# Sums of local attention weights: overlapping columns added on GpSimd before TensorE sums them, with a new time table

## The reference

```python
# local: a query at j looks at keys j-32 .. j+31
logits = jnp.where(win & valid, q . k * scale, NEG)
out_local  = softmax(logits) @ v
# global: each query looks at every 64th key (128 of them)
out_global = softmax(q . k[:, ::64] * scale) @ v[:, ::64]
out = (out_local + out_global) @ w_out + b_out
```

## Time and profile before

| | |
|---|---|
| median of 3 runs | 3730.59 us (3727.56 to 3732.28) |
| the profiled execution | 3731.16 us, span 3728.6 us |
| mean granted clock of PE over the span | 0.991 of full speed |
| PE / DVE / ACT / POOL busy in the span | 98% / 62% / 43% / 52% |
| PE matmul pieces | 28480 |
| attention phase | begins at about 1220 us |

### The profile page before, as it was taken

How to read it: one execution, slowest core, us unless ns; L and a number is a source line. 1 busy time by engine, 2 the same in 40 slices (tenths; PEclk the granted TensorE clock), 3 DMA queues, 4 the chain that set the end, 5 groups by cost and what they waited for, 6 DMA issues and landing times.

```text
span 3728.6 us, 77177 instructions
## 1 busy us (share of the span) xinstructions
PE 3652.7 (98%) x28480; PEld 2682.6 (72%) x28480; DVE 2318.0 (62%) x5354; ACT 1596.2 (43%) x3110; POOL 1938.8 (52%) x3091
## 2 busy tenths in 40 slices
PE   8999999999998899999999999999999999999997
PEld 6888888888886567766667666666766666666665
DVE  4333333333334577777777777777777777777774
ACT  3222222222222355555555555555555555555553
POOL 0000000000000477777777777777777777777776
PEclk9999999999998999999999999999999999999999
DMA  4554554554457666666666666666666666666641
GB/s 146 203 189 160 191 198 163 179 202 171 167 211 185 131 141 144 139 145 152 151 141 141 141 150 150 144 140 143 150 146 145 141 149 147 141 145 143 150 111 40
DMA packets 420883, 571.20 MB, mean 153 GB/s; under 512 B 41656, under 2 KB 187208, under 8 KB 420568
## 3 DMA queue, kind: packets, MB, share of 16 engines
q1 hardware_dynamic: 412024, 564.79, 58.0%
q10 hardware_dynamic: 8256, 2.16, 0.3%
q0 software_dynamic: 288, 0.08, 0.0%
HBM read 361.59 MB, written 203.23 MB: 151 GB/s over the span
## 4 chain that ended last, share of the span: by engine, by line
PE 63%; POOL 1%; ACTq 1%; ACT 0%; DVE 0%; issue 0%; POOLq 0%
PE ps_misc L1056 19%; PE ps_max L974 10%; PE ps_sc L996 6%; PE ps_o L1028 6%; PE ps_max L977 5%; PE ps_s L1028 4%; PE ps_sc L1010 4%; PE ps_o L1040 3%; PE ps_s L1034 3%; PE ps_sc L1065 1%; ACTq L842 1%; PE ps_sc L983 1%; PE ps_sc L1004 1%; ACT qk L819 0%; POOL rsb L752 0%
## 5 line engine op out<-in xcount | busy, mean ns | idle before, releaser
L885 DVE TENSOR_REDUCE mx<-ps_max 128x2 f32<-128x256 f32 (+1 forms) x1365 | 485.5, 356 | 494.2 <-PE ps_max L977 471.0
L819 ACT ACTIVATE qk<-ps_sc 128x384 f32<-128x384 f32 (+1 forms) x1024 | 419.3, 461 | 669.1 <-PE ps_sc L996 662.3
L451 PE MATMUL po<-ht_hi,w_both 128*128 128x512 f32 x2048 | 655.1, 394 | 1.5 <-ACT ht_hi L276 1.5
L886 DVE TENSOR_REDUCE mx<-ps_max 128x2 f32<-128x384 f32 (+1 forms) x1365 | 612.6, 449 | 0.0
L451 PEld LDWEIGHTS po<-ht_hi,w_both 128*128 128x128 f32 x2048 | 385.7, 188 | 81.3 <-ACT ht_hi L276 1.8
L761 POOL TENSOR_SCALAR_AFFINE_SELECT qk<-qk 128x512 f32<-128x512 f32 (+1 forms) x512 | 299.9, 586 | 196.0 <-ACT qk L819 196.0
L451 PE MATMUL po<-ht_lo,w_both 128*128 128x512 f32 x1024 | 399.8, 390 | 0.0
L832 ACT ACTIVATE v<-ps_sc 128x512 f32<-128x512 f32 x512 | 298.6, 597 | 151.1 <-PE ps_sc L1010 149.3
L977 PE MATMUL ps_max<-mask,ident_b 128*128 128x192 bf16 x2048 | 352.7, 254 | 0.0
L764 POOL TENSOR_SCALAR_AFFINE_SELECT qk<-qk 128x512 f32<-128x512 f32 x512 | 326.4, 637 | 35.0
L810 ACT ACTIVATE xb<-xb,nmb,rsb 128x512 f32<-128x512 f32 x384 | 311.2, 811 | 74.3 <-POOL nmb L754 74.3
(11 more groups left out here) (154 smaller groups left out, 7677.5 us busy)
## 6 DMA issues: line engine op xcount, KB each, us to landing
w_both<-q_hi_d SPq DMA_DIRECT2D x256, 256.0 KB
ks<-k_hi_d SPq DMA_DIRECT2D x128, 288.0 KB
xb<-in_L_attn_x SPq DMA_DIRECT2D x132, 256.0 KB, 3.4
q_lo_d<-o_lo SPq DMA_DIRECT2D x32, 1024.0 KB, 8.7
k_lo_d<-o_lo SPq DMA_DIRECT2D x32, 1024.0 KB, 10.1
w_both<-q_lo_d SPq DMA_DIRECT2D x128, 256.0 KB
vw<-v_d SPq DMA_DIRECT2D x128, 256.0 KB, 2.9
out<-xb SPq DMA_DIRECT2D x128, 256.0 KB, 3.3
```

What stands on the lines that cost most here:

```text
L451: last = nc.tensor.matmul(po[o % 6][:], wa[:, k, o * P:(o + 1) * P], ha[u][:, k, :], start=start, stop=stop)
L819: nc.scalar.activation(p_loc[:, i, 2 * hp:2 * hp + 2, lo:MW], ps_sc[n % 2][:, 0:2 * MW].rearrange("p (h n) -> p h n", h=2)[:, :, lo:MW], A ...
L885: nc.vector.tensor_reduce(mx[s % 2][:, 1, h:h + n, tile], ps_max[:, b:b + n, MW:MW + NGLOB], axis=AX.X, op=ALU.max)
L886: last = nc.vector.tensor_reduce(mx[s % 2][:, 0, h:h + n, tile], ps_max[:, b:b + n, 0:MW], axis=AX.X, op=ALU.max)
```

## The change

POOL, after both maskings of tile i > 0, adds the last 64 queries of tile i - 1 and the first 64 of tile i, which are the same queries, into a new tile `p_sum` (3 x 4 heads x 64, in free columns of the buffer `qk0`), and counts up `s_added`. PE's `pvl` keeps all products for `ps_o`. The sums are no longer taken with each tile: with tile 1 come those of tiles 0 and 1 (the 64 queries of each that no other tile covers, together 128, and 64 of `p_sum`), with tile 3 those of tiles 2 and 3 (64 of tile 2, 128 of `p_sum`, and the last 128 of tile 3), with the last piece its 64. That is 128 + 64 + 64 + 128 + 128 + 64 = 576 columns per head, in six groups where there were five. `pvl` 1 and 3 wait for `s_added`. ACT, before it overwrites tile i of `p_loc`, waits for the `pvl` that read it last (1 or 3) and, for tile 1, for the additions. All due times of the table are new.

```diff
@@ -595,6 +595,7 @@
         ks = [stacks.keys(g) for g in range(GROUPS)]
         ones, mask, ident, ident_b, mhalf = stacks.ones, stacks.mask, stacks.ident, stacks.ident_b, stacks.mhalf
         p_loc = qk0[:].rearrange("p a n -> p (a n)")[:, 0:16 * MW].bitcast(F32).rearrange("p (i h n) -> p i h n", i=4, h=4)
+        p_sum = qk0[:].rearrange("p a n -> p (a n)")[:, 16 * MW:16 * MW + 12 * WIN].bitcast(F32).rearrange("p (i h n) -> p i h n", i=3, h=4)
         vw = [sb(f"vw{g}", [P, 4, P], F32) for g in range(GROUPS)]
         vl = [sb(f"vl{g}", [WIN, P], F32) for g in range(GROUPS)]
         vg = [sb(f"vg{g}", [P, P], F32) for g in range(GROUPS)]
@@ -626,7 +627,7 @@
         y_stored = [sem(f"y_stored{i}") for i in range(TILES)]
         max_scored, max_taken = sem("max_scored"), sem("max_taken")
         sc_scored, sc_exped = sem("sc_scored"), sem("sc_exped")
-        early_cut, loc_masked = sem("early_cut"), sem("loc_masked")
+        early_cut, loc_masked, s_added = sem("early_cut"), sem("loc_masked"), sem("s_added")
         pvl_done, pvgs_done, pvgo_done = sem("pvl_done"), sem("pvgs_done"), sem("pvgo_done")
         sums_step = sem("sums_step")
         o_copied, ol_done, og_done, o_sum = sem("o_copied"), sem("ol_done"), sem("og_done"), sem("o_sum")
@@ -649,20 +650,20 @@
             if n > 0:
                 eng.wait_ge(s, n)
 
-        MAXIMA = (-12.81, -11.26, -10.56, -9.74, -8.61, -7.49, -6.9, -6.1)
-        TAKEN = 0.12
-        SCORES = (("mt", 0, -4.23), ("loc", 0, -0.65), ("loc", 1, 0.87), ("loc", 2, 1.16), ("loc", 3, 5.18),
-                  ("last", 0, 5.77), ("glob", 0, 1.84), ("glob", 1, 2.44), ("glob", 2, 2.81), ("glob", 3, 5.4))
-        VALUES = (("pvl", 0, 3.67), ("pvl", 1, 3.73), ("pvl", 2, 6.64), ("pvl", 3, 7.14), ("pvl", 4, 7.63),
-                  ("pvgs", 0, 8.23), ("oc", 0, 8.33), ("sums", 0, 9.08), ("pvgo", 0, 9.82), ("rglob", 0, 9.46),
-                  ("og", 0, 9.75), ("rloc", 0, 13.65), ("ol", 0, 14.11), ("osum", 0, 14.12))
-        LATE = (("ot", (21.84, 18.21, 19.35, 14.23)), ("otl", (21.91, 22.79, 18.96, 14.23)))
-        OUT_AT = ((9.01, 9.05, 10.17, 10.85), (8.33, 9.39, 9.57, 9.91))
-        FFN_AT = ((24.77, 24.89, 26.47, 26.72), (24.83, 25.25, 25.81, 25.91))
-        TAIL = (("outa", (10.03, 9.93)), ("outs", (11.88, 10.87)), ("rs0", (12.88, 12.9)), ("y", (13.42, 15.19)),
-                ("ya", (13.77, 15.33)), ("x1", (15.58, 17.37)), ("rs1", (15.82, 17.46)), ("x1n", (17.75, 18.99)),
-                ("tr", (19.4, 19.48)), ("trl", (19.76, 19.98)), ("ffna", (27.15, 27.29)), ("ffns", (27.74, 28.27)),
-                ("rs2", (28.11, 28.38)), ("z", (33.81, 35.69)), ("za", (34.37, 35.77)))
+        MAXIMA = (-13.0339, -11.6822, -10.4258, -9.7281, -8.598, -7.58, -6.9132, -6.069)
+        TAKEN = 0.244
+        SCORES = (("mt", 0, -4.6645), ("loc", 0, -0.6178), ("loc", 1, 0.8309), ("loc", 2, 1.2942), ("loc", 3, 5.0147),
+                  ("last", 0, 5.5892), ("glob", 0, 1.885), ("glob", 1, 2.0223), ("glob", 2, 2.579), ("glob", 3, 6.096))
+        VALUES = (("pvl", 0, 3.5335), ("pvl", 1, 4.2772), ("pvl", 2, 6.4924), ("pvl", 3, 6.5459), ("pvl", 4, 8.0969),
+                  ("pvgs", 0, 8.3105), ("oc", 0, 8.264), ("sums", 0, 8.7344), ("pvgo", 0, 9.4196), ("rglob", 0, 9.7303),
+                  ("og", 0, 10.1161), ("rloc", 0, 14.2168), ("ol", 0, 14.293), ("osum", 0, 14.4318))
+        LATE = (("ot", (21.7751, 17.0825, 18.4842, 14.8026)), ("otl", (21.8109, 23.0519, 20.0382, 14.9253)))
+        OUT_AT = ((8.8077, 8.9602, 10.1365, 10.5371), (9.2322, 9.4608, 9.6397, 10.1425))
+        FFN_AT = ((24.4874, 24.8324, 26.4422, 26.5671), (24.8758, 25.5695, 25.6924, 26.1212))
+        TAIL = (("outa", (11.1558, 10.2756)), ("outs", (12.1528, 11.3768)), ("rs0", (12.2821, 11.912)), ("y", (13.2603, 13.5629)),
+                ("ya", (13.8542, 14.5427)), ("x1", (15.8153, 16.8242)), ("rs1", (16.1468, 17.4515)), ("x1n", (17.9124, 18.3468)),
+                ("tr", (19.3168, 19.8798)), ("trl", (19.7958, 20.0908)), ("ffna", (26.7516, 26.6579)), ("ffns", (27.3399, 27.9282)),
+                ("rs2", (28.5786, 28.7788)), ("z", (34.4086, 35.7999)), ("za", (34.5167, 37.0638)))
 
         def timeline():
 
@@ -762,6 +763,9 @@
                                            base=WIN - 1 if i == 0 else -1, channel_multiplier=-1).then_inc(early_cut, 1)
                         pool.wait_ge(early_cut, s * 4 + i + 1)
                         pool.affine_select(late, late, [[0, 4], [-1, P]], ALU.is_ge, 0.0, base=0, channel_multiplier=1).then_inc(loc_masked, 1)
+                        if i > 0:
+                            pool.wait_ge(loc_masked, 5 * s + i + 1)
+                            pool.tensor_tensor(p_sum[:, i - 1, :, :], p_loc[:, i - 1, :, P:MW], p_loc[:, i, :, 0:WIN], ALU.add).then_inc(s_added, 1)
                     if name == "last":
                         pool.wait_ge(sc_exped, unit(s, "last", 0) + 1)
                         pool.affine_select(p_last[:], p_last[:], [[0, 4], [1, WIN]], ALU.is_ge, 0.0,
@@ -811,7 +815,9 @@
 
                 def item(name, s, i):
                     if name == "loc":
-                        at_least(act, pvl_done, 5 * (s - 1) + i + 1)
+                        at_least(act, pvl_done, 5 * (s - 1) + (2 if i < 2 else 4))
+                        if i == 1:
+                            at_least(act, s_added, 3 * (s - 1) + 2)
                         lo = WIN if i == 0 else 0
                         for hp in range(2):
                             n = unit(s, "loc", i, hp)
@@ -1015,18 +1021,27 @@
                             at_least(pe, og_done, s)
                             at_least(pe, sums_step, 4 * (s - 1) + 1)
                         pe.wait_ge(loc_masked, 5 * s + i + 1)
-                        for dst, vals in ((ps_o, vw[g]), (ps_s, None)):
+                        if i in (1, 3):
+                            pe.wait_ge(s_added, 3 * s + i)
+                        for h in range(4):
+                            rows, head = slice(h * DH, (h + 1) * DH), slice(h * DH, (h + 1) * DH)
+                            if i < 4:
+                                x0, w = (0, P) if i == 0 else (P * i - WIN, MW)
+                                last = nc.tensor.matmul(ps_o[rows, x0:x0 + w], vw[g][:, i, head], p_loc[:, i, h, MW - w:MW],
+                                                        start=i == 0, stop=False, skip_group_check=True)
+                            else:
+                                last = nc.tensor.matmul(ps_o[rows, CHUNK - WIN:CHUNK], vl[g][:, head], p_last[:, h, :],
+                                                        start=False, stop=True, skip_group_check=True)
+                        halves = ps_s[:].rearrange("p (t b n) -> p t b n", b=2, n=WIN)
+                        parts = {1: ((halves[:, 0:2, 0, :], p_loc[:, 0:2, :, WIN:P]), (halves[:, 0, 1, :], p_sum[:, 0, :, :])),
+                                 3: ((halves[:, 2, 0, :], p_loc[:, 2, :, WIN:P]), (halves[:, 1:3, 1, :], p_sum[:, 1:3, :, :]),
+                                     (ps_s[:, CHUNK - P:CHUNK], p_loc[:, 3, :, WIN:MW])),
+                                 4: ((ps_s[:, CHUNK - WIN:CHUNK], p_last[:]),)}.get(i, ())
+                        for n, (sums, windows) in enumerate(parts):
                             for h in range(4):
-                                if i < 4:
-                                    x0, w = (0, P) if i == 0 else (P * i - WIN, MW)
-                                    lhs = ones[:, 0, :] if vals is None else vals[:, i, h * DH:(h + 1) * DH]
-                                    rhs = p_loc[:, i, h, MW - w:MW]
-                                else:
-                                    x0, w = CHUNK - WIN, WIN
-                                    lhs = ones[0:WIN, 0, :] if vals is None else vl[g][:, h * DH:(h + 1) * DH]
-                                    rhs = p_last[:, h, :]
-                                last = nc.tensor.matmul(dst[h * DH:(h + 1) * DH, x0:x0 + w], lhs, rhs,
-                                                        start=i == 0, stop=i == 4 and dst is ps_o, skip_group_check=True)
+                                window = windows[:, :, h, :] if len(windows.shape) == 4 else windows[:, h, :]
+                                last = nc.tensor.matmul(sums[h * DH:(h + 1) * DH], ones[0:windows.shape[0], 0, :], window,
+                                                        start=i == 1 and n == 0, stop=False, skip_group_check=True)
                         last.then_inc(pvl_done, 1)
                     if name == "pvgs":
                         pe.wait_ge(sc_exped, unit(s, "glob", 3) + 1)
```

## The result

The changed kernel took 3684.55 us (median; 3683.75 to 3685.69), the kernel before, run beside it, 3731.44 us. The ratio is 0.9876 with a 95% interval of 0.9859 to 0.9893: 47 us less. Forecast were 3692 us, 39 us less.

What follows compares the result with a forecast made beforehand. PE, busy 98% of the span, was taken to bound the kernel. Columns -42, transposed maxima +8, exponential wait -8 and output projection +3 gave -39 us, from 3731 to 3692 us; range 3672 to 3722.

Steps and rivals of the forecast that it cites:

- The columns: Local softmax sums on PE: fewer columns save 0.33 us a step, 42 us over 128 steps.
- Rival C: Sums on PE: small matmuls cost more than their columns, gain 14 us instead of 42, kernel at 3720 us; 5%.
- The additions: Three a step on GpSimd, 0.75 us plus 0.07 us waiting each, 2.4 us a step; cost to the kernel 3 us.
- waiting left for GpSimd: GpSimd, steady stretch: 3.1 us a step of waits for other engines shrink to 0.4 us, close to full.
- the first output projection: PE, once in each of 32 chunks: waits about 0.1 us for GpSimd's low part, 3 us; called the tightest place.
- tile 3 costs nothing: PE's wait for tile 3's sums: 2.1 us of slack covers the 0.8 us addition, with at least 1.0 us over.
- A: Rival: GpSimd too late for each chunk's output projection; PE waits 2.3 us a chunk, 74 us, kernel at 3763 us; 9%.
- The table: New order on PE at two places in every step: +8 us and -8 us, nothing on balance.
- the transposed maxima: PE, moved ahead of tile 0's value products, not covered by a strip change: 0.06 us a step, 8 us lost.
- the wait ahead of the fourth global score: PE's wait for ScalarE's exponentials, 8.0 us in the steady stretch, goes as the score moves later: -8 us.

Runs made afterwards that it cites:

- e2: The kernel before with the new due times alone, no saved columns and no additions: 3716.77 us, ratio 0.9966.
- e3: The changed kernel without GpSimd's three additions a step and the waits for them, other exponentials standing in for the added columns: 3676.93 us, ratio 0.9862.
- e4: The changed kernel with the same 576 columns for the sums cut into nine groups of 64 instead of six of 64 and 128: 3684.72 us, ratio 0.9883.
- e8: The changed kernel with the addition of tile 3 alone made twice, 0.8 us more a step: 3747.98 us, ratio 1.005.
- e1: The changed kernel with the due times of the kernel before, so fewer columns and the additions without the new table: 3685.65 us, ratio 0.9882.
- e11: The changed kernel, new table throughout, with the last piece padded by zeros from 64 to 128 rows: 3672.8 us, ratio 0.9849.
- e5: The changed kernel with new due times in its first eight steps and old ones after, chunk tail at old times throughout: 3683.06 us, ratio 0.9872.
- e6: e5 with the last piece of each chunk padded by zeros from 64 to 128 rows: 3669.57 us, ratio 0.9842.
- e9: e5 with the new due times in the first four steps alone, where no chunk tail runs yet: 3674.91 us, ratio 0.9856.
- e10: e9 with the last piece padded to 128 rows and PE's wait for the zeros put at their first use: 3662.13 us, ratio 0.9826.
- e7: The changed kernel with each of GpSimd's three additions made twice, 2.4 us more a step: 3926.16 us, ratio 1.0526.

## Why the prediction was right, and where it was off

**The columns.** Forecast 0.33 us a step, 42 us. The steady step fell by 0.315 us, 40.4 us in 128 steps, but that number has the table and the additions in it as well. What isolates the columns is e2 against e3, which share the table and have no additions: 0.320 us a step (19.298 to 18.978), 40 us between the medians. Taken piece by piece, the time from the start of each piece of the local sums to the next start falls from 1.64 to 1.33 us a step, by 0.315, with either table. So 64 columns cost 0.105 us, where the timeline's two decimals gave 0.11. Rival C falls: e4 shows 14 ns a piece and no change in time. The floor of about 25 ns a matmul in the Trainium skill (TensorE: Matmul & The Clock Gate, "Wait — 56ns, not 53.3ns?") does not hold for pieces in different column strips, by the same 14 ns; within one strip the starts lie four times as far apart, some 55 ns, so no run tries the floor there. (Reckoned from the prediction's own groups the floor would give 0.15 us a step and not 0.14.)

**The additions.** Forecast 0.75 us and 0.07 us of waiting; measured 0.735 and 0.08. Forecast 0.4 us of waiting left for GpSimd in a step, measured 0.8: the forecast started from the four largest waits, 3.1 us a step, and all six make 3.4, which leaves 0.7. Forecast a wait of 0.1 us a chunk at the first output projection, 3 us; measured 0.1 us, 3.2 us for the steady stretch of e3. That tile 3 costs nothing holds for the steady stretch; PE waits for an addition once between 1330 and 3640 us, and that is at 3617.7 us, in the last steps:

```profile
PE ps_o L1030 <- POOL qk L768: 1.5, 1, 1.5
```

What the prediction left out are the two ends: against e3 the last seven steps lost 3.3 us to the additions, half of it in this one wait, and the first four 1.4, which no row of mine covered, because I read the steady stretch only. So the additions cost 8 us, where I had 3.

**The rival that ends slower.** A was given 9%. Its mechanism is real and very near: 0.8 us more a step on GpSimd and the kernel is slower than before. Its price there was underestimated, since I followed one place where PE meets GpSimd and e8 shows three.

**The table.** This is the term whose size was wrong: it was forecast to bring nothing on balance, +8 us for the transposed maxima and -8 us for the wait ahead of the fourth global score, and it brought 12 us (e2).

In the steady stretch the two halves are about right one by one. The same items in the same succession, in e1 and in the changed kernel (from the mask products of the `max` ahead of the value products of tile 0 to those of the next `max` behind the sums of tile 1, with the transposed maxima between):

```profile
2046.25 0.34 PE L983 MATMUL ps_max<-mask,ident_b 128*128 128x192 bf16 x2
...
2048.01 0.34 PE L983 MATMUL ps_max<-mask,ident_b 128*128 128x192 bf16 x2
```

```profile
2052.95 0.34 PE L983 MATMUL ps_max<-mask,ident_b 128*128 128x192 bf16 x2
...
2054.81 0.34 PE L983 MATMUL ps_max<-mask,ident_b 128*128 128x192 bf16 x2
```

1.76 us and 1.86 us; in the mean of all steps that have this succession the maxima cost 0.08 us more in the new order, 10 us in 128 steps (forecast 0.06 and 8). And PE's idle time between step 8 and step 120 is 7.4 us before and 0.0 in e2 and after. But the wait all but goes in e1 as well (0.7 us of idle time). It comes where ScalarE takes long to issue the two small DMAs of the maxima. The kernel before, ScalarE's timeline and PE's:

```profile
2096.81 2.15 ACTq L842 DMA_DIRECT2D w_both<-mt  x2
2099.06 0.87 ACT L819 ACTIVATE qk<-ps_sc 128x384 f32<-128x384 f32 x2 [2.29 <-PE ps_sc L996]
```

```profile
2099.61 0.50 PE L1010 MATMUL ps_sc<-w_both,ks 99*128 99x512 f32 x1 [0.73 <-ACT qk L819]
```

Two issues take 1.15 us mostly and 2.15 here; the exponentials queued behind them come late. In the kernel before 15 of the attention phase's 254 issues took over 0.9 us, in e1 only 4, and PE waited 6.7 us less, which goes with the 0.07 us a step that e1 gained beyond its columns. The kernels with the new table that GpSimd doesn't hold up (after, e2, e3, e4, e11) have 15 to 21 such issues, and PE waits for none of them between step 8 and step 120: there the order, not luck, removes the wait. Why the old table has fewer once the columns are gone was not tried; e5, e6, e9 and e10, which run the old table in the steady stretch, have few as well (5 to 11). So with the columns the new order finds little left to remove, and only its price remains: it takes 0.074 us a step against e1.

What the table does bring, 9 to 12 us in the first four steps, was no term of my sum at all. There the wait ahead of the fourth global score comes in every step, 1.0 to 1.6 us long; the order takes away 3 to 4 us of idle time, and 5 to 9 us of busy time with the half clock that followed some of these waits.

That PE's idle time brings the drop of the clock has good support. The drop comes with the waits in before and e1, and is absent in e2 and after. e9, whose fifth step has the old times, has such a wait again (1.45 us at 1278 us) and 3.4 us at half clock behind it. And e7 and e8 come near to a test: they have the new table, and only additions more than the changed kernel. PE waits for these in the first four steps, and the half clock is back, for 14 us in e7 and 7 in e8. e8's wait and the stretch behind it:

```profile
1269.58 0.87 PE L1033 MATMUL ps_o<-qk,vw 128*32 128x192 f32 x8 [1.29 <-POOL qk L771]
```

```profile
1272.00:1276.00 4.00, 4.00 (x31) 1.58 (x30) 0.89 (x2) 1.35 (x3) 2.68 (x4) 0.50 1.08 210
```

Which idle time does it stays open, for its length does not tell: three waits of 1.14 to 1.15 us in before had no drop behind them, one of 1.15 us in e1 had 3.4 us of half clock behind it, and in e5 and e6 PE stands idle twice for 2.0 to 2.1 us at their seam, with 3.4 us of half clock behind the first in e5 and none behind the others. e6 there (the idle time ends at 1299.59 us):

```profile
1296.00:1300.00 4.00, 1.87 (x10) 1.23 (x9) 2.21 (x6) 0.89 (x2) 0.41 (x1) 1.00 0.48 146
```

No run puts in a wait alone and varies it.

**The sum.** By the medians, before to e2 to e3 to the changed kernel: the table -12 us (forecast 0), the columns -40 (forecast -42), the additions +8 (forecast +3). That the total came within 8 us is in part luck: the additions cost 5 us more than forecast and the table gave 12 us that were not forecast, and these two errors work against each other.

## What to carry to other kernels

Where an engine is full, read the price of a change from gaps between starts, not from durations: eight pieces of 0.2 to 0.3 us lay 0.11 us apart, and the sum came out within 2 us. When work is moved to an engine that has room, count its waits for others per step against the new work, and look for every place where the full engine meets it: here 2.4 us fitted into 3.4 us, and 3.2 would have lost the whole gain. And read the first and last steps by themselves: an order that costs nothing in the steady stretch cost 9 to 12 us at the start, in idle time and at half clock, and a table for the start and another for the rest beat either.

## What the runs showed of the hardware

Padding 64 rows to 128 made PE faster: between 64-row and 128-row matmuls in column strips it pays 0.11 us, which is gone when both have 128 rows, with the columns costing the same. Starts of fp32 pieces in four column strips beside each other lay 14 ns apart on average (e4), with no change in the kernel's time for nine groups in place of six. In the first steps the granted clock fell from 1.00 to 0.50 for 7 to 14 us at idle times of PE of 1.1 to 1.6 us (before, e1, e7, e8), with other waits in the steps around them; yet others of 1.14 to 1.15 us (before) had nothing behind them, and those of 2.0 to 2.1 us (e5, e6) 3.4 us or nothing, so the length of one idle time does not tell. An issue of the same small DMA by ScalarE took about 0.5 us mostly and up to 2 us at times, 4 to 21 times in 254, depending on the kernel; what makes it long stays open.
